# First stage of a long-convolution block on one core: in four units, a last tap moved from VectorE to ScalarE and GpSimd

## What is computed

```python
z = rmsnorm(u, pre_norm_w) @ in_proj_w.T            # u: layernorm of the input; 256 -> 768 channels
zc = z.transpose(0, 2, 1)
z_pre = conv(zc, short_w) + short_b                 # 3 taps per channel, along the tokens, causal
x2, x1, v = jnp.split(z_pre, 3, axis=1)
h = jnp.sum(residues * jnp.exp(log_poles * t), axis=1)   # long filter, 16 poles per channel
xv = x1 * v
yconv = irfft(rfft(xv, n=2 * L) * rfft(h, n=2 * L))[..., :L]
y = (yconv + xv * D_skip) * x2
y = y.transpose(0, 2, 1) @ out_proj_w.T + u
```

## Time and profile before

| | |
|---|---|
| median of 3 runs | 1090.52 us (1090.23 to 1091.44) |
| the profiled execution | 1089.94 us, of it the profile's span 1088.2 us |
| TensorE busy | 98% of the span |
| VectorE, ScalarE, GpSimd busy | 81%, 66%, 27% |
| TensorE clock granted | 0.999 of full speed |
| the first stage | up to about 190 us |

### The profile page before, as it was taken

One profiled execution on the slowest core, in us unless ns is written; L12 is line 12 of the kernel. 1 busy time (PEld: TensorE's weight loads), 2 busy tenths in 40 slices (PEclk: granted clock), 3 DMA queues, 4 the chain that ended last, 5 costly groups with the idle time before them and its releaser, 6 DMA issues.

```text
span 1088.2 us, 25029 instructions
## 1 busy us (share of the span) xinstructions
PE 1061.7 (98%) x9012; PEld 1007.5 (93%) x9012; DVE 881.3 (81%) x2321; ACT 714.5 (66%) x1605; POOL 298.4 (27%) x575
## 2 busy tenths in 40 slices
PE   8899999899999999999999999999999999999998
PEld 7777788678989999999999999989999999999997
DVE  7999998763788877788888877898888888887776
ACT  7878887674455766666666666665666666666644
POOL 6677784730001111111111111111111211111111
PEclk9999999999999999999999999999999999999999
DMA  3347989994743333333333333443333333333000
GB/s 128 118 126 223 269 231 216 385 329 49 169 74 41 52 57 59 50 59 49 51 52 55 60 61 58 108 108 40 60 50 59 50 51 52 57 66 52 30 20 30
DMA packets 113067, 104.93 MB, mean 96 GB/s; under 512 B 7616, under 2 KB 103808, under 8 KB 112688
## 3 DMA queue, kind: packets, MB, share of 16 engines
q1 hardware_dynamic: 111712, 100.77, 42.4%
q0 software_dynamic: 736, 2.51, 0.7%
q10 hardware_dynamic: 496, 0.05, 0.0%
HBM read 77.84 MB, written 32.80 MB: 102 GB/s over the span
## 4 chain that ended last, share of the span: by engine, by line
PE 66%; DVE 6%; issue 2%; ACT 1%; POOL 0%; DMA 0%; SPq 0%; POOLq 0%; DVEq 0%; ACTq 0%
PE ps_ring L1509 34%; PE ps_w L1509 15%; PE ps_m L1509 9%; PE ps_o L1509 4%; PE ps_rt L1524 2%; DVE base L1331 1%; PE ps_w L1519 1%; DVE bn L1235 1%; PE ps_m L1575 1%; DVE prod L1278 0%; DVE ht_l L1247 0%; DVE pt_l L1247 0%; POOL sc L1087 0%; DMA base<-in_w 0%; DVE yrow L1470 0%
## 5 line engine op out<-in xcount | busy, mean ns | idle before, releaser
L1087 POOL TENSOR_TENSOR sc<-sc,neg_half 128x2 f32<-128x2 f32 x127 | 94.7, 745 | 677.7 <-DVE sc L1459 406.5
L1152 ACT ACTIVATE gate<-ps_ring 128x256 f32<-128x256 f32 x192 | 73.0, 381 | 125.8 <-PE ps_ring L1509 124.9
L1173 ACT ACTIVATE hid<-ps_ring,b1s 128x256 f32<-128x256 f32 x256 | 112.4, 484 | 29.0 <-PE ps_w L1509 13.5
L1509 PE MATMUL ps_ring<-mt_l,wl_h 128*128 128x256 f32 x640 | 125.5, 277 | 2.6 <-DVE mt_l L1247 2.6
L1509 PE MATMUL ps_ring<-mt_h,wl_h 128*128 128x256 f32 x640 | 125.4, 277 | 2.0 <-DVE prod L1278 1.4
L1509 PE MATMUL ps_ring<-mt_h,wl_l 128*128 128x256 f32 x640 | 124.9, 276 | 0.0
L1247 DVE TENSOR_TENSOR ht_l<-hid,ht_h 128x256 fp32r<-128x256 f32 x256 | 103.1, 423 | 16.2 <-ACT ht_h L1177 10.2
L1509 PE MATMUL ps_ring<-xt_h,we_h 128*128 128x256 f32 x512 | 103.3, 283 | 2.7 <-DVE prod L1278 2.4
L1278 DVE TENSOR_TENSOR prod<-ps_ring,gate 128x256 f32<-128x256 f32 x192 | 80.8, 421 | 24.4 <-ACT gate L1152 20.0
L1509 PE MATMUL ps_ring<-xt_h,we_l 128*128 128x256 f32 x512 | 100.0, 277 | 0.0
L1509 PE MATMUL ps_ring<-xt_l,we_h 128*128 128x256 f32 x512 | 100.0, 276 | 0.0
(11 more groups left out here) (201 smaller groups left out, 2752.7 us busy)
## 6 DMA issues: line engine op xcount, KB each, us to landing
toep_scratch<-taps_scratch SPq DMA_DIRECT2D x30, 512.0 KB, 7.9
toep<-toep_scratch SPq DMA_DIRECT2D x30, 512.0 KB, 9.5
xa<-in_x SPq DMA_DIRECT2D x16, 512.0 KB, 4.9
x_scratch<-x2c SPq DMA_DIRECT2D x16, 512.0 KB, 3.7
x2s<-x_scratch SPq DMA_DIRECT2D x32, 256.0 KB, 6.9
xa_c<-in_x SPq DMA_DIRECT2D x32, 256.0 KB, 2.6
xb_c<-in_x SPq DMA_DIRECT2D x32, 256.0 KB, 2.6
yin<-seq SPq DMA_DIRECT2D x124, 64.0 KB, 6.2
```

Source lines behind the costliest of these rows:

```text
L1087: nc.gpsimd.tensor_tensor(sc[:, to], sc[:, to], neg_half[:, 0, 0:CC], ALU.pow).then_inc(S[done], 1)
L1152: nc.scalar.activation(gate[rows_of, m % 2], ring[m % RING][rows_of, 0], ACT.Gelu_apprx_tanh).then_inc(S["gate_done"], 1)
L1173: nc.scalar.activation(hid[:, m % HIDS], block_of, ACT.Gelu, bias=b1s[:, m:m + 1]).then_inc(S["hid_done"], 1)
L1509: mm = nc.tensor.matmul(out, lhs(a, kk), rhs(b, kk), start=(j == 0), stop=(closed and j == len(todo) - 1))
```

## The change

A helper `beside(u)` says for which positions of unit u tap 2 is scaled by ScalarE and added by GpSimd: i=4 and i=5 in units 0 to 3 (`LAST_POWERS` = 3), i=4 alone in the others. `beside_until(u)` counts them over the units before u, and takes the place of the plain unit numbers in all waits on `x2_done` and `tap_extra`. `x2_tap` has two blocks in place of one, 2 KB more per partition, and the ring of powers has 12 tiles in place of 16, 2 KB less. VectorE's tap 2 at i=5 is gone in the four units. GpSimd's second add comes right behind the first. Lines of the changed kernel are up to 10 higher than before.

```diff
--- before.py
+++ after.py
@@ -141,7 +141,7 @@
     ident, neg_half, seq = v["ident"], v["neg_half"], v["seq"]
     norm_scale, norm_shift = v["norm_scale"], v["norm_shift"]
     x2_dram, taps_dram = v["x2_dram"], v["taps_dram"]
-    POWERS = 16
+    POWERS = 12
     FIRST_POWERS, LAST_POWERS = 18, 3
     ROWS_HERE = 2
     OVER, SLOTS, XBUFS = TAPS - 1, 4, 3
@@ -174,7 +174,7 @@
         zt = [sb(ctx, f"zt_{s}", [P, 2, KB, TA], F32R) for s in "hl"]
         conv = sb(ctx, "conv", [P, ZB - KB, OVER + TA])
         x2c = sb(ctx, "x2c", [P, 2, KB, OVER + TA])
-        x2_tap = sb(ctx, "x2_tap", [P, TA])
+        x2_tap = sb(ctx, "x2_tap", [P, KB, TA])
         xv = sb(ctx, "xv", [P, KB, TA])
         ps_t = [ps(ctx, f"ps_t{b}", [P, TA]) for b in range(KB)]
         ps_x = [ps(ctx, f"ps_x{j}", [P, CA, P]) for j in range(KB)]
@@ -206,6 +206,15 @@
         def opens(u):
 
             return u % (UA // B) == 0
+
+        def beside(u):
+
+
+            return (4, 5) if u <= LAST_POWERS else (4,)
+
+        def beside_until(u):
+
+            return sum(len(beside(n)) for n in range(u))
 
         def steps():
             return range(-2, UA + 2)
@@ -267,7 +276,7 @@
                     sp.wait_ge(S["taps_ready"], KB + 1)
                     sp.dma_start(taps_dram.rearrange("(p k) t -> p k t", k=KB), taps[:]
                                  ).then_inc(S["taps_out"], 16)
-                sp.wait_ge(S["x2_done"], u + 1)
+                sp.wait_ge(S["x2_done"], beside_until(u + 1))
                 sp.wait_ge(S["conv_done"], ZB * (u + 1))
                 sp.dma_start(x2_dram[:, :, u * TA:(u + 1) * TA], x2c[:, u % 2, :, 0:TA]).then_inc(x2_out[u % 2], 16)
             sp.wait_ge(S["taps_out"], 16)
@@ -354,7 +363,7 @@
                 nc.gpsimd.tensor_copy(pair[:, :, 0:OVER], over).then_inc(S["carried"], 1)
 
             def carry_x2(u):
-                pool.wait_ge(S["x2_done"], u + 1)
+                pool.wait_ge(S["x2_done"], beside_until(u + 1))
                 pool.wait_ge(S["conv_done"], ZB * (u + 1))
                 wait(pool, x2_out[1 - u % 2], 16 * ((u + 1) // 2))
                 over = x2c[:, u % 2, :, TA:]
@@ -375,10 +384,11 @@
                         carry(n, j)
                         if j == 0 and n > 0:
                             carry_x2(n - 1)
-                    pool.wait_ge(S["conv_done"], ZB * n + 5)
-                    pool.wait_ge(S["tap_extra"], n + 1)
-                    nc.gpsimd.tensor_tensor(sums_of(0, n, 2), sums_of(0, n, 2), x2_tap[:], ALU.add
-                                            ).then_inc(S["x2_done"], 1)
+                    for k, i in enumerate(beside(n)):
+                        pool.wait_ge(S["conv_done"], ZB * n + i + 1)
+                        pool.wait_ge(S["tap_extra"], beside_until(n) + k + 1)
+                        nc.gpsimd.tensor_tensor(sums_of(k, n, 2), sums_of(k, n, 2), x2_tap[:, k], ALU.add
+                                                ).then_inc(S["x2_done"], 1)
 
         @block.scalar
         def _(act):
@@ -423,9 +433,9 @@
                                          bias=sbias[:, m:m + 1]).then_inc(S["opened"], 1)
                 nc.scalar.activation(sums_of(m, u, 0), slot(b)[:], ACT.Identity, scale=sw[:, m, 0:1],
                                      bias=sbias[:, m:m + 1]).then_inc(S["tap_done"], 1)
-                if i == 4:
-                    wait(act, S["x2_done"], u)
-                    nc.scalar.activation(x2_tap[:], slot(b)[:], ACT.Copy, scale=sw[:, m, 2:3]
+                if i in beside(u):
+                    wait(act, S["x2_done"], beside_until(u))
+                    nc.scalar.activation(x2_tap[:, m], slot(b)[:], ACT.Copy, scale=sw[:, m, 2:3]
                                          ).then_inc(S["tap_extra"], 1)
 
             def gate_rows(u, j):
@@ -533,16 +543,16 @@
                         dve.wait_ge(S["tap_done"], ZB * n + i + 1)
                         if n == 0:
                             dve.wait_ge(S["opened"], i + 1)
-                        if i == 4:
-                            dve.wait_ge(S["tap_extra"], n + 1)
-                        add_tap(n, i, 1, "conv_done" if i == 4 else "mid_done")
+                        if i in beside(n):
+                            dve.wait_ge(S["tap_extra"], beside_until(n) + i - 3)
+                        add_tap(n, i, 1, "conv_done" if i in beside(n) else "mid_done")
                     if i in (1, 3):
                         if valid(n + 1, UA):
                             turned_low(n + 1, i // 3)
                     elif valid(n + 3, UA):
                         measure(n + 3, i // 2 if i < 3 else i - 2)
-                    if valid(n, UA) and i != 4:
-                        dve.wait_ge(S["mid_done"], (ZB - 1) * n + (i if i < 4 else 4) + 1)
+                    if valid(n, UA) and i not in beside(n):
+                        dve.wait_ge(S["mid_done"], ZB * n - beside_until(n) + (i if i < 4 else 4) + 1)
                         add_tap(n, i, 2, "conv_done")
                     if i in (0, 3):
                         long_taps(powers_at(n, i))
```

## The result

The changed kernel takes 1093.17 us (median of 15 runs, 1091.87 to 1096.45), the kernel before 1091.07 us (15 runs, 1089.18 to 1092.0). The ratio is 1.0025 with a 95% interval of 1.0017 to 1.0034: the change makes the kernel slower by 1.9 to 3.7 us. The forecast was 3.4 us slower.

A forecast was written before the change was run, and what follows sets the result against it. TensorE, busy 98%, was taken as the bound, with VectorE full in units 0 to 3. Late chain 3.05 plus `taps` 0.4 gave 3.45, rounded to 3.4, on the median of 1090.52: 1093.9 us, range 1090.8 to 1095.3.

The forecast's parts named there:

- the late transposes: Sign on TensorE behind unit 3: the transposes of `xv` near 71.88 come near 75.3 us.
- the waits at i=3 of 0.5 to 1.2 us: Sign on VectorE in units 1 to 3: waits on ScalarE's `conv` at i=3, about 0.5 to 1.2 us each.
- the new add, step on GpSimd: GpSimd, units 0 to 3: the second add ahead of the row chain costs what the present one costs, 1.31 us.
- slack before VectorE waits: VectorE's tap 1 of i=3 could start at 60.87 but starts at 61.60: 0.73 us, taken for all three steps.
- slip of a unit: Units 1, 2 and 3: 1.31 us later less 0.73 slack, so each slips 0.58 us instead of gaining 0.65.
- three slips, up to unit 3: At i=3 of unit 3, after three units: 1.74 us late.
- row chain behind unit 3: GpSimd in step 3: chain starts 1.74 + 1.31 = 3.05 us late, and everything behind moves with it.
- `taps` beside the chain: GpSimd's row chain beside VectorE's pairs of `taps` at i=0: 0.13 us a pair, 0.4 over three units.
- ScalarE's tap: ScalarE, units 0 to 3: one more `x_tap` of 0.57 us, covered by the 2.06 us wait; cost 0.
- The first: ScalarE's wait at `zn`, units 1 to 3: row chain stays covered, at most 2.6 us faster, 1087.9 us; chance 0.06.
- The second: GpSimd's row chain: pairs of `taps` stop it in full, 4.75 us slower, 1095.3 us; chance 0.10.
- The third: Later reserve, for instance the handover to the second stage, returns up to 3 us: 1090.5 to 1092.7 us; chance 0.16.

The follow-up runs named there:

- e2: Kernel before with a ring of 12 powers and one more GpSimd add on a spare tile in units 0 to 3; stage 164.84 us, ratio 1.0018.
- e6: Changed kernel without GpSimd's new add, ScalarE's second scaled tap and VectorE's shorter list kept; stage 161.93 us, ratio 0.9992.
- e8: Changed kernel run and traced once more, no edit; stage 164.46 us, ratio 1.0019 to the kernel before.
- second pair: Kernel before and changed kernel each traced once more, no edit; stages 162.67 and 164.46 us, medians 1091.28 and 1092.99 us.
- e1: Changed kernel with the new add of i=5 put behind the next unit's first `xv` instead of ahead of the row chain; stage 165.06 us, ratio 1.0030.
- e5: Changed kernel with GpSimd's row chain of the next step between the two adds; stage 163.09 us, ratio 1.0015.
- e9: Kernel before with VectorE's pair of `taps` at i=3 moved between tap 1 and tap 2; stage 160.29 us, 1089.71 us, ratio 0.9976.
- e11: Changed kernel with the row chain between the two adds and VectorE's pair of `taps` at i=3 moved ahead of tap 2; stage 163.03 us, ratio 0.9996.

## Why the prediction was right, and where its sizes were off

The forecast was 1093.9 us with a range of 1090.8 to 1095.3 and a chance of 0.73 on slower; 1093.17 was measured. The sign and the mechanism hold: the new add stands ahead of the row chain, ScalarE's `zn` waits for the chain, VectorE waits for ScalarE, and its saved tap is lost in that wait. e2 and e6 show it from both sides, and unit 1 of e8 has the wait at i=3. Of the signs named, VectorE's gaps between 40 and 50 us and the late transposes came; the waits at i=3 of 0.5 to 1.2 us came once (e8), units 1 and 2 grew by 0.17 us and not 0.6, and the transposes came at 73.06 and not near 75.3. The steps below were wrong in size, and one cost was taken as nothing that is not. The stage became 1.5 to 1.8 us longer, where 3.45 was forecast; that the whole kernel came nearer to the forecast is luck as far as the runs show.

| step, as forecast | forecast | measured |
|---|---|---|
| the new add, step on GpSimd | 1.31 | 0.97; 1.05 in unit 3 |
| slack before VectorE waits | 0.73 | 0.82 |
| slip of a unit | 0.58 | 0.17 |
| three slips, up to unit 3 | 1.74 | 0.49 |
| row chain behind unit 3 | 3.05 | 1.54 |
| `taps` beside the chain | 0.4 | under 0.05 (second pair 0.2) |
| the stage | 3.45 | 1.47 (second pair 1.79) |

*The add.* "It costs what the present one costs" took the step from the add of i=4 to the row chain. The two adds take 2.29 from the first to the chain (42.07 to 44.36) against 1.32 for one: the new one costs 0.97. In e1 and e5, where the two stand apart, it takes 1.10 us, and the one of i=4 1.28 to 1.29. The slip of a unit is a small difference of two such numbers, 0.97 - 0.82 = 0.15 (0.17 by the stores) in place of 1.31 - 0.73, so an error of a quarter in a term became a factor of three.

*The slack.* The 0.13 us from a ScalarE end to the VectorE start was read at another wait. Here it is 0.04 (49.70 to 49.74), which makes the slack 61.60 - 60.74 - 0.04 = 0.82.

*Unit 3.* The first transposes start 0.34 us earlier in this trace (25.61 against 25.95). Against them the adds of unit 3 start 65.32 - 65.17 + 0.34 = 0.49 late, which is the three slips, and the chain 67.63 - 66.43 + 0.34 = 1.54; the 1.05 between is the new add, where 1.31 was forecast. TensorE's transposes follow it (73.06), as forecast, and nothing is given back.

*ScalarE's tap.* "Cost taken: 0" was argued from ScalarE's wait of 2.06 us, which comes behind the tap. But VectorE waits for ScalarE ahead of that wait as well, at i=0 and i=5, and there the tap comes first. The trace of the change has this wait (43.93, 0.49 us). Beside the late chain it costs little, since VectorE has time to lose; with the chain on time it takes 1.3 of the 1.9 us that the saved taps are worth.

*The rivals.* The first, full gain with the chain covered, is now bounded: even without any add the change gains 0.6 us, not 2.6. The second, every pair stopping the chain for its whole length, did not occur: units 1 to 3 of the change have one such stop, of 0.2 us, in the second trace (e8). By the rule of the Trainium skill behind it (SBUF — State Buffer, section Who interferes with whom), a VectorE instruction with two SBUF inputs contends with a GpSimd instruction that reads SBUF. The traces agree: the pair takes 1.6 us beside `xv` and 0.60 once it is moved away (e9), and one chain operation beside the pair 0.39 in place of 0.20 (e2). The third, part of it given back, is not seen in the stage (chain 1.54 late, stage 1.47 longer).

What stays open: why e11 is no faster than e5; why the new add, and e2's, are shorter than the add of i=4; and where the rest of the total comes from. The ratio's 2.7 us (medians: 2.1) is 0.6 to 1.2 more than the stage's 1.5. The two traces of each kernel do not show where, since the later stages scatter by 1.5 to 2 us on their own.

## What to carry to other kernels

Before work is moved to an engine with much idle time, look where in its list it lands and who waits for what stands behind it: GpSimd was busy for 7.99 of 10 us and waited beside that, and one more microsecond ahead of its row chain was worth more than VectorE's saving. A wait covers only work whose result nobody needs before that wait. And before a full engine is relieved, look for its operations that are longer than their like: the pair at 1.6 us in place of 0.6 was a bigger reserve than the tap, for two moved lines.

## What the runs showed that was not expected

Two adds of one shape need not cost the same. GpSimd in e1, the new add of i=5 and then the add of i=4:

```profile
49.39 1.10 POOL L377 TENSOR_TENSOR x2c<-x2c,x_tap 128x512 f32<-128x512 f32 x1
...
53.69 1.28 POOL L377 TENSOR_TENSOR x2c<-x2c,x_tap 128x512 f32<-128x512 f32 x1 [0.64 <-DVE x2c L515]
```

Neither follows another add, so it is not the row of two that makes the new one short. It is 1.10 in e5 too (46.42), and e2's add on the spare tile takes 1.04. What makes the difference, no run shows. Who starts first seems to matter between VectorE's pair of `taps` and GpSimd's short operations: in e2 the pair starts at 45.73 and the operation at 45.74 takes 0.39 us in place of 0.20, and so in two more units; in the change the operation starts at 45.56, the pair at 45.58, and both take what they always take.
